# Finding an edge's place in the ring: squared distances on TensorE, two steps ahead, in place of transposed one-hots

## The reference: one graph-attention layer

```python
h = relu(layernorm(x))
h = (h @ W_node.T).reshape(N, 4, 32)
e = (edge_attr @ W_edge.T).reshape(E, 4, 32)
att = sum(concat([h[src], h[tgt], e]) * a, axis=-1)      # per edge and head
att = where(att > 0, att, 0.2 * att)
m = maximum(segment_max(att, tgt), 0)
ex = exp(att - m[tgt])
denom = segment_sum(ex, tgt) + (E - deg)[:, None] * exp(-m)
out = x + segment_sum((ex / denom[tgt])[:, :, None] * h[src], tgt)
```

## Time and profile before

| | us |
|---|---|
| median of 3 runs (lowest, highest) | 2956.02 (2949.07, 2960.83) |
| the profiled execution, its own time | 2958.49 |
| its span, first to last instruction | 2956.7 |
| busy: POOL / DVE / PE / ACT | 1576.9 / 1558.5 / 1394.2 / 796.3 |
| mean granted TensorE clock | 0.618 of full |

### The profile page before, as it was taken

How to read it: one execution, slowest core, us unless ns; L and a number is a source line. 1 busy time by engine, 2 the same in 40 slices (tenths; PEclk the granted TensorE clock), 3 DMA queues, 4 the chain that set the end, 5 groups by cost and what they waited for, 6 DMA issues and landing times.

```text
span 2956.7 us, 39019 instructions
## 1 busy us (share of the span) xinstructions
PE 1394.2 (47%) x9599; PEld 1292.3 (44%) x9600; DVE 1558.5 (53%) x4449; ACT 796.3 (27%) x2329; POOL 1576.9 (53%) x1674
## 2 busy tenths in 40 slices
PE   4424544544545445444455464454544544544465
PEld 4414444434445444344344353444433433534455
DVE  4345554554545555545555445455454555454568
ACT  4412222222222222222222222222222222222233
POOL 6525555555555555555655555556555555555530
PEclk7656665656655656656556556565565666565667
DMA  7352322222222223222222232222222222222220
GB/s 210 81 185 64 81 66 63 78 69 64 78 66 80 67 64 80 67 65 78 68 70 73 67 80 67 65 77 69 66 77 65 79 67 65 81 66 64 80 67 22
DMA packets 119885, 224.74 MB, mean 76 GB/s; under 512 B 40373, under 2 KB 80181, under 8 KB 113093
## 3 DMA queue, kind: packets, MB, share of 16 engines
q0 software_dynamic: 53440, 113.99, 16.5%
q1 hardware_dynamic: 65565, 110.07, 11.5%
q10 hardware_dynamic: 848, 0.35, 0.1%
HBM read 180.28 MB, written 43.98 MB: 76 GB/s over the span
## 4 chain that ended last, share of the span: by engine, by line
another core or an unknown queue 38%; DVE 23%; issue 17%; PE 12%; ACT 5%; DVEq 3%; ACTq 1%; DMA 0%; SPq 0%
PE bank_z L1185 5%; DVE vals L835 5%; DVE bank_rn L715 4%; DVE rows_mem L719 3%; PE bank_w L1243 3%; DVE s_sum L791 2%; ACT onehot_bits L1084 2%; PE bank_rn L1203 2%; PE bank_t L1210 1%; DVE lk L804 1%; DVEq L80 1%; ACT s_live L1078 1%; ACTq L80 1%; DVE den L880 1%
## 5 line engine op out<-in xcount | busy, mean ns | idle before, releaser
L487 POOL DMA_INDIRECT gath<-h_table,idx x1621 | 1531.7, 945 | 1260.1 <-issue 458.1
L1084 ACT COPY onehot_bits<-bank_t 128x1024 bf16<-128x1024 bf16 x209 | 211.5, 1012 | 1279.3 <-remote 915.9
L1220 PE MATMUL bank_s<-s_live,onehot_bits 128*128 128x24 bf16 x1672 | 76.1, 179 | 842.4 <-ACT onehot_bits L1084 759.5
L1220 PEld LDWEIGHTS bank_s<-s_live,onehot_bits 128*128 128x128 bf16 x1672 | 61.1, 102 | 891.4 <-issue 891.4
L1243 PE MATMUL bank_p<-vals,onehot 128*128 128x137 f32 x1664 | 404.2, 435 | 0.3
L1243 PEld LDWEIGHTS bank_p<-vals,onehot 128*128 128x128 f32 x1664 | 377.4, 328 | 4.9 <-DVE vals L835 0.2
L1210 PE MATMUL bank_t<-ident_b,onehot_bits 128*128 128x128 bf16 x1672 | 199.2, 293 | 358.6 <-DVE onehot_bits L727 310.6
L1210 PEld LDWEIGHTS bank_t<-ident_b,onehot_bits 128*128 128x128 bf16 x1672 | 163.5, 139 | 381.9 <-DVE onehot_bits L727 325.3
L1243 PE MATMUL bank_w<-vals,onehot 128*128 128x137 f32 x1664 | 320.8, 367 | 0.0
L1243 PEld LDWEIGHTS bank_w<-vals,onehot 128*128 128x128 f32 x1664 | 298.4, 266 | 0.0
L727 DVE SCALAR_TENSOR_TENSOR onehot_bits<-bank_w,tables,zz 128x1024 bf16 (+1 forms) x209 | 268.3, 1284 | 27.4 <-issue 12.9
(11 more groups left out here) (167 smaller groups left out, 1851.2 us busy)
## 6 DMA issues: line engine op xcount, KB each, us to landing
ef<-in_edges SPq DMA_DIRECT2D x52, 1024.0 KB
out_x<-x_all SPq DMA_DIRECT2D x210, 128.0 KB
gath<-h_table,idx POOLq DMA_INDIRECT x1621
x_all<-in_x SPq DMA_DIRECT2D x14, 448.0 KB, 6.1
out_x<-x_all SPq DMA_DIRECT2D x14, 448.0 KB
h_table<-gath SPq DMA_DIRECT2D x12, 462.0 KB
resets<-ef SPq DMA_DIRECT2D x8, 416.0 KB
flag_rows<-resets SPq DMA_DIRECT2D x52, 64.0 KB
```

The source lines that it names most:

```text
L487: e.indirect_dma_start(gath[:, q * GPS + g, t * ROW:(t + 1) * ROW], None, table, bass.IndirectOffsetOnAxis(idx[:, q, g * TILES + t:g * TIL ...
L1084: e.copy(onehot_t[:, :, :], bank_t[:, :].bitcast(BF16).rearrange("p (t c) -> p t c", c=P)).then_inc(s_e, 1)
L1220: ins = e.matmul(s2e[buf][:, t * S2W:(t + 1) * S2W], onehot_t[:, t, :], s2_live[:, :], start=True, stop=True)
```

## The change

TensorE no longer transposes VectorE's one-hot. A place in the ring is a number of 7 bits, split into a high part (bits 4 to 6) and a low part (bits 0 to 3). For each edge the squares and the values of both parts are prepared once (`dst_terms`, 4 rows a group, bf16); for each ring place the same with factors -2 (`place_terms`). One matmul over 18 rows then gives, for 128 ring places x 512 edges, the squared distance of edge and place: 0 on a match, at least 1 elsewhere. ScalarE's Relu(1 - distance) turns that into the transposed one-hot. VectorE's own one-hot, widened for the products, stays. A group takes two such matmuls (`distances(0)`, `distances(1)`) through the same `bank_t`, and two ScalarE passes of 512 columns (`matched(0)`, `matched(1)`). They are for the step *two* ahead of the one at hand: `onehot_t` of the next step is ready before this step begins. Its core:

```diff
+            def distances(k, sel, at, count=None):
+                if count is not None:
+                    wait(e, s_e, count)
+                e.matmul(bank_t[:, :], place_sb[:, bass.ds(sel, P)],
+                         terms_sb[:, bass.ds(at + k * 512, 512)], start=True, stop=True
+                         ).then_inc(s_t, 1)
...
                 for q in range(2):
-                    turn_one_hot(1 - q, s_2)
                     if beside[q][0]:
                         beside[q][0]()
-                    spread_s2(1 - q, s_2)
+                    spread_s2(1 - q, s_2, (h4, h6)[q])
+                    distances(0, *ahead)
...
                     ins.then_inc(s_b, 1)
+                    distances(1, *ahead, (h5, h7)[q])
```

```diff
-                    transposed(s_2)
+                    matched(0, (h5, h7)[q])
                     factors(s, s_1)
                     widened(1 - q, s, s_2)
+                    matched(1, (h6, h8)[q])
...
-            def transposed(count):
+            def matched(k, count):
                 wait(e, s_t, count)
-                e.copy(onehot_t[:, :, :], bank_t[:, :].bitcast(BF16).rearrange(
-                    "p (t c) -> p t c", c=P)).then_inc(s_e, 1)
+                e.activation(onehot_t[:, k * 4:(k + 1) * 4, :], bank_t[:, :].rearrange(
+                    "p (t c) -> p t c", c=P), ACT.Relu, bias=one[:, :], scale=-1.0
+                    ).then_inc(s_e, 1)
```

Around it, in the first stage:

```diff
+            e.wait_ge(d_store, 16 * CHUNKS)
+            e.tensor_single_scalar(dst_low, dst_rows, LOW, op=ALU.bitwise_and).then_inc(n_bits, 1)
+            wait(e, n_bits, 1)
+            e.tensor_single_scalar(dst_rows, dst_rows, HIGH, op=ALU.bitwise_and).then_inc(n_bits, 1)
...
+            chain(e.tensor_single_scalar(sel_row, g_row, GPS - 1, op=ALU.bitwise_and))
+            chain(e.tensor_scalar(sel_row, sel_row, float(P), None, ALU.mult))
+            chain(e.tensor_single_scalar(at_row, g_row, 2, op=ALU.arith_shift_right))
+            chain(e.tensor_scalar(at_row, at_row, float(GROUP), None, ALU.mult))
+            for k in range(2):
+                for i, row in enumerate((sel_row, at_row)):
+                    chain(e.tensor_copy(pe_rec[:, :, 2 * k + i], row[:, k + 2:k + 2 * PAIRS + 3:2]))
```

More of the change, by code:

```diff
@@ L368, in _ @@
             load_edges(0)
-            for c in range(CHUNKS):
-                e.dma_start(out[:, c * CHUNK:(c + 1) * CHUNK, :], x_all[:, c * CHUNK:(c + 1) * CHUNK, :]
-                            ).then_inc(d_fill, 16)
+            e.wait_ge(d_terms_out, 16 * TERMS)
+            wait(e, n_terms, TERMS + 2)
+            for q in range(2):
+                load_terms(q, q)
             def landed(b, i, q, last_turn):
@@ L515, in _ @@
             chain(e.memset(eps[:, :], 4.0 * EPS))
+            chain(e.memset(one[:, :], 1.0))
+            e.memset(place_sb, 0.0).then_inc(n_place, 1)
+            chain(e.memset(place_row[:, 0:2, :], 1.0))
+            wait(e, n_const, 2)
+            chain(e.tensor_copy(place_high, ring[32:33, 0:P]))
+            chain(e.tensor_single_scalar(place_low, place_high, LOW, op=ALU.bitwise_and))
+            chain(e.tensor_single_scalar(place_high, place_high, HIGH, op=ALU.bitwise_and))
+            for k, part in enumerate((place_high, place_low)):
+                times, square = place_row[:, 2 + k, :], place_row[:, TERMS + k, :]
+                chain(e.tensor_scalar(times, part, -2.0, None, ALU.mult))
+                ins = e.scalar_tensor_tensor(out=square, in0=times, scalar=0.25, in1=times,
+                                             op0=ALU.mult, op1=ALU.mult)
+                if k == 0:
+                    chain(ins)
+            ins.then_inc(n_place, 1)
             def statistics(c):
@@ L1104, in _ @@
             live_s2(w_0, 2)
-            transposed(1)
+            matched(0, 1)
+            matched(1, 2)
             wait(e, s_oh, 1)
             e.copy(onehot[0][:, :, :], onehot_b[0][:, :, :]).then_inc(s_of, 1)
+            matched(0, 3)
+            matched(1, 4)
             z_maxima(0, 0)
@@ L1262, in _ @@
             turn_z(0)
-            turn_one_hot(0, 1)
-            spread_s2(0, 1)
+            e.wait_ge(d_place, 16 * (GPS + 1))
+            e.wait_ge(d_terms, 32)
+            sel_0, at_0, sel_1, at_1 = load(nc, e, pe_rec[0:1, 0:1, :].rearrange(
+                "p a c -> p (a c)"), [(GPS - 1) * P, (RING - 1) * GROUP] * 2)
+            distances(0, sel_0, at_0)
+            distances(1, sel_0, at_0, 1)
+            spread_s2(0, 1, 2)
+            distances(0, sel_1, at_1)
+            distances(1, sel_1, at_1, 3)
             maxima(0)
```

114 lines of the change are left out of this document (89 added, 25 removed).

## The result

The changed kernel takes 2991.6 us (median of 20 runs, 2973 to 3014), the kernel before 2965.1 (20 runs, 2949 to 2974). The ratio is 1.0093, 95% interval 1.0075 to 1.0111: slower by 0.9%. I had forecast 2893 us and 60% for faster.

A forecast was written before the change was run, and what follows sets the result against it. Gathers were taken to hold TensorE's signals, leaving gaps between bursts; (2.6 - 0.4 - 3.6) x 49 = -69, +6 for the first stage, gave -63, and 2958.5 - 63 - 2.5 = 2893 us, range 2740 to 3000.

The forecast's parts named there:

- gathers hold TensorE's signals: While gathers run, TensorE's signals are held until 1.8 us (after 8 gathers) or 3.0 us (after 16) behind them.
- rival 4: No signal is held; gathers are the limit, 40 us a block for 53.9: about 2280 us, chance 3%.
- Gap after step 2: Pause in gathers after a block's first sixteen: matched(1), unseen, exponentials and vals follow the hold in turn, +2.6 us a block.
- Gap after step 3: Pause in gathers after the next eight: ScalarE's pass ahead of ab takes 0.62 for 1.01 us, -0.4 us a block.
- Gap after step 4: Pause before the next block's first gather: scans start 4.05 us earlier, -3.6 us a block, bounds -4.05 and -1.95.
- the flush: The moment behind a burst of gathers when held TensorE signals come through; 1.8 us after 8 gathers, 3.0 after 16.
- It needs a gap under 1.8 us: Condition for rival 2: the pause before the next block's first gather is shorter than 1.8 us.
- rival 2: Next block's first gather precedes the flush, step 4's signals stay held: 57.8 us a block for 53.9, 3150 us, chance 10%.
- First stage: Work ahead of the loop: VectorE's extra integer passes and small ones add +6 us, once.
- the step of 6.19 us: Where no gathers run, a step takes 6.19 us instead of 13.5; read as evidence that gathers delay signals.

The follow-up runs named there:

- e4_nogath: The changed kernel without the gathers of the loop over blocks: 2060.1 us, beside 2143.7 for the kernel before.
- e5_after: The changed kernel itself, run again where no signal is held: 2152.7 us beside 2142.4 for the kernel before (ratio 1.0047).
- e7_nogath_b: The kernel before without the gathers of the loop over blocks and the waits for their arrival: 1735.8 us.
- s1_flush: The changed kernel, each block's first gather also waiting for TensorE's maxima of step 4: 2976.2 us beside 3070.6 for the kernel before (0.9681).
- t1b_flush_early: The changed kernel, each block's first gather also waiting for TensorE's second distances product of step 4: 2964.7 us beside 3069.3 for the kernel before (0.9668).
- h4_order: The changed kernel with written holds, ScalarE's second pass behind the next step's exponentials, factors ahead of the first: 3242.2 us beside 2959.0 for the kernel before (1.0951).

## Why the prediction was wrong, point by point

- *What bounds the kernel: gathers hold TensorE's signals.* The gaps are right for the chips of the result. That gathers are what holds was read from the order in time, and no run without them met such a chip. For it speaks the trace of the result itself: its last two blocks, behind the last gather, take 36.1 and 39.1 us, as the blocks of `e4_nogath` on a chip that holds nothing (35.7 to 39.0). Where the kernel before takes 2143 us the same gathers hold nothing, and my rival 4 is true to its reason: gathers are the limit at 40.0 us a block, as its 32 x 1.25. I had 2280 for it and 3%. It lacked the first stage and the end, which are shorter there as well: its first gather of the loop comes at 139.0 us for 205.4, and behind the last one are 45.7 us for 106.5. By the Trainium skill, "SBUF — State Buffer", section on the two separate sides, a DMA and a compute engine cannot slow each other at SBUF. By that nothing would be held; the chips of one kind agree with it (`e5_after` has no remote wait for L1181), those of the other don't (1223.5 us).
- *Gap after step 2, +2.6.* Right: 7.55 for 5.05. The row of `matched(1)`, `unseen`, exponentials and `vals` stands behind the hold as described.
- *Gap after step 3, -0.4.* Right: 3.42 for 3.81. Its reading in the kernel before was not quite: there it is TensorE's work that is late, more than a signal. The 32 edge products ahead of the transposes take 6.84 us (from 1540.37 on) for 3.63 in `e7_nogath_b`, and the transposes start at 1547.06, behind the eighth gather.
- *Gap after step 4, -3.6.* This is the step that failed. The size was near in 17 gaps of 47 (2.05 to 2.15 us, where I had about 2), but it ended where two events cross. The forecast put the next block's first gather 11.5 us into the burst in four blocks of five, and the flush at 9.7 + 1.8 = 11.5 as well, and then priced the gap as if the flush always came first. "It needs a gap under 1.8 us" stood under rival 2, with 10% and 3150 us, as a choice between no block and every block. It came in every third block: 15 x (58.85 - 52.15) = 100 us. The row of `turn_z` that the forecast read takes 1.04 us, and where it takes that in the changed kernel, the gather comes first.
- *First stage, +6.* Nearly right, 7.9.
- *Not in the sum: the blocks behind the last gather.* Three blocks compute when no gather runs. There the chain of steps is the time, and the change makes it longer: the last two blocks take 36.1 and 39.1 us for 32.4 and 31.9, the whole end 120.1 for 106.5, +13.6. I had quoted for the step of 6.19 us and had not asked what it becomes; the sum had this term at nothing.

Together: without a split 48 blocks would have given 48 x (52.15 - 54.02) = -90, and 2956.7 - 90 + 7.9 + 13.6 = 2888, close to the forecast; the 100 us of the splits lead to 2988 of the 2991.7 measured. That the forecast of 2893 would then have been close is in part luck, since +13.6 at the end, which the sum lacked, stands against gaps that shrank by 90 us where it had 69. That the race makes the splits is shown by the sorted blocks, where less than 0.2 us separates all from none, and by `s1_flush` and `t1b_flush_early`, in which a wait behind the flush leaves none. That the wait costs 1.1 us and so gives back half of its gain is read from its rows. Open is what decides whether a chip holds signals, why the gap after step 4 differs between two that do, and what decides the clock at `turn_z`. Not tried: to release the first gather by VectorE's signal some 0.3 us later, which by the rows would put the gaps at 1.95 to 2.45 (an estimate) without the way from TensorE to GpSimd; and the change with its second product ahead of the sums.

## What to carry to other kernels

When a forecast ends with two events a few tenths of a microsecond apart, and the order of the two decides over many microseconds, it is not one case but a mixture: work out the price of each order and ask how much the distance varies from block to block. Here TensorE's clock alone moved it by 0.3 us, enough for both orders: a duration taken from one row of TensorE holds for one clock. When a bound hides a chain, measure the chain with the bound removed, as here by leaving out the gathers: it grew by 6.4 us a block, some 2.9 of them by a lower clock (an estimate), and the stretches where the bound is absent (the last blocks) pay for it in full. And run the kernel before beside every experiment: here its own time said first that an experiment had met another bound.

## What the runs showed of the hardware

The same program takes 2143 or 2959 to 3071 us, by whether TensorE's work comes through while gathers run; the gather itself takes 946 ns in both. Where it is held, it is not only signals that are late. From some 8 us into a burst in `h4_order` (1444.7, the burst from 1436.65) and 15 us into one in the changed kernel (the burst from 1588.84) TensorE's own matmuls come one by one, in the latter 2.1 us apart, and nine in a row only 2.9 us behind the last gather (which ends at 1608.5):

```profile
1603.68 0.17 PE L1286 MATMUL bank_z<-w_edge_bd,ef 128*128 128x8 f32 x1 [0.18 <-issue]
1605.77 0.17 PE L1286 MATMUL bank_z<-w_edge_bd,ef 128*128 128x8 f32 x1 [1.93 <-issue]
1607.88 0.17 PE L1286 MATMUL bank_z<-w_edge_bd,ef 128*128 128x8 f32 x1 [1.93 <-issue]
1609.98 0.17 PE L1286 MATMUL bank_z<-w_edge_bd,ef 128*128 128x8 f32 x1 [1.92 <-issue]
1611.38 1.88 PE L1286 MATMUL bank_z<-w_edge_bd,ef 128*128 128x8 f32 x9 [1.23 <-issue]
```

They wait for nothing that the profile shows. That instructions arrive late by DMA is unlikely: the page's part 3 has these packets for the whole span, the same in a trace without holds (`e5_after`):

```profile
q8 instruction: 9, 0.15, 0.0%
q14 instruction: 23, 0.19, 0.0%
```

A burst of 8 gathers lets the first signals through: in the changed kernel the pass ahead of `ab` is seen 7.0 to 8.6 us into the burst of step 4, but behind a split block only at 9.2 to 11.4. What VectorE writes to GpSimd came through during a burst: the `rescale` that ends at 1525.46 releases the second eight gathers of its block, and the ninth follows the eighth at 1528.06 without a gap. Where GpSimd stands waiting, a gather starts 1.0 to 1.1 us behind the start of the instruction ahead of its release (1517.02 to 1518.06, 1568.90 to 1570.01). The granted clock of TensorE moves whole stretches of a step: eight products of `turn_z` take 1.04 or 1.87 us, sixteen of the sums 2.12 or 4.02.
